# Cross-attention and low-rank FFN in one launch: the seam between the two stages rebuilt, weights split earlier, first and last tiles reordered

## What is computed

```
x = x + softmax(clip((LN(x) Wq + bq)(ctx Wk + bk)^T * 32**-0.5, +-10000)) (ctx Wv + bv) Wo + bo
x = x + gelu(LN(x) U1 V1 + b1) U2 V2 + b2        # U1 512x128, V1 128x2048, U2 2048x128, V2 128x512
```

## Time and profile before

| | |
|---|---|
| median of 3 runs | 580.68 us (578.64 to 581.20) |
| profiled execution | 577.34 us, span 575.5 us |
| mean granted PE clock | 0.997 |
| busy share of the span | PE 96%, PEld 81%, DVE 84%, POOL 64%, ACT 54% |
| moved by DMA | 50.36 MB |

### The profile page before, as it was taken

The page is one execution under the profiler, slowest core; times in us unless marked ns, Lnnn a source line. Parts: engine busy times, 40 slices in busy tenths (PEclk is TensorE's granted clock), DMA queues, the critical chain, the costliest instruction groups (busy, mean ns, idle before and its releaser), DMA issues.

```text
span 575.5 us, 11999 instructions
## 1 busy us (share of the span) xinstructions
PE 554.8 (96%) x4804; PEld 464.2 (81%) x4804; DVE 482.8 (84%) x697; ACT 308.7 (54%) x510; POOL 366.6 (64%) x286
## 2 busy tenths in 40 slices
PE   8999999999999999999987997999999999999996
PEld 8787878888988898888865675888888888888884
DVE  4778989888988898888779968888979797978675
ACT  3464454445444545444456543757575766666652
POOL 2787767777676777677565564757566656565561
PEclk9999999999999999999989999999999999999999
DMA  8422353222323123220412431012121212101012
GB/s 311 163 79 75 110 202 112 93 70 71 101 92 112 54 77 112 92 75 20 148 56 74 129 112 72 0 75 73 74 73 67 81 56 91 57 19 56 18 61 86
DMA packets 25263, 50.36 MB, mean 87 GB/s; under 512 B 2936, under 2 KB 3064, under 8 KB 24824
## 3 DMA queue, kind: packets, MB, share of 16 engines
q1 hardware_dynamic: 24920, 49.07, 24.8%
q10 hardware_dynamic: 288, 0.52, 0.3%
HBM read 32.49 MB, written 16.78 MB: 86 GB/s over the span
## 4 chain that ended last, share of the span: by engine, by line
PE 78%; DVE 9%; DMA 6%; ACT 2%; POOL 2%; issue 2%; SPq 1%; POOLq 0%; DVEq 0%
PE bank L965 46%; PE ps_s L965 15%; PE bank L1040 5%; PE ps_s L1014 4%; PE bank L1056 4%; DMA xs<-in_x 4%; PE bank L1081 2%; PE bank L986 2%; DVE ss L748 1%; DVE smax L757 1%; DVE ssum L762 1%; DMA fw<-y_between 1%; DVE stats L687 1%; POOL ss L399 1%; DVE hs_r L824 1%
## 5 line engine op out<-in xcount | busy, mean ns | idle before, releaser
L471 POOL TENSOR_TENSOR hs_r<-ss,hs_r 128x512 fp32r<-128x512 f32 x63 | 90.3, 1434 | 90.1 <-ACT hs_r L667 89.5
L646 ACT ACTIVATE ss<-ps_s,once 128x512 f32<-128x512 f32 x128 | 87.9, 689 | 67.5 <-PE ps_s L965 64.0
L965 PE MATMUL ps_s<-p1t_r,v_r 128*128 128x512 f32 x384 | 112.2, 401 | 0.3 <-DVE p1t_r L813 0.3
L965 PE MATMUL bank<-hs_r,u_r 128*128 128x512 f32 x384 | 109.3, 393 | 0.7 <-DVE hs_r L824 0.7
L399 POOL TENSOR_TENSOR ss<-ss,smax 128x1232 f32<-128x1232 f32 x32 | 75.1, 2346 | 49.6 <-DVE smax L757 49.5
L965 PE MATMUL bank<-zt_r,wqo_r 128*128 128x256 f32 x768 | 98.7, 284 | 1.1 <-DVE zt_r L708 1.1
L965 PE MATMUL bank<-wqo_r,ot_r 128*128 128x512 f32 x384 | 98.9, 407 | 0.7 <-DVE ot_r L770 0.5
L965 PEld LDWEIGHTS bank<-zt_r,wqo_r 128*128 128x128 f32 x768 | 92.5, 188 | 2.8 <-DVE zt_r L708 1.3
L965 PEld LDWEIGHTS bank<-hs_r,u_r 128*128 128x128 f32 x384 | 72.0, 188 | 17.9 <-DVE hs_r L824 1.1
L965 PEld LDWEIGHTS bank<-wqo_r,ot_r 128*128 128x128 f32 x384 | 70.9, 191 | 16.6 <-DVE ot_r L770 0.9
L407 POOL TENSOR_TENSOR ss<-ss,rsum 128x1024 f32<-128x1024 f32 x32 | 61.5, 1922 | 35.7 <-DVE rsum L764 35.5
(11 more groups left out here) (86 smaller groups left out, 817.9 us busy)
## 6 DMA issues: line engine op xcount, KB each, us to landing
xs<-in_x SPq DMA_DIRECT2D x64, 256.0 KB, 3.5
y_between<-xs SPq DMA_DIRECT2D x32, 256.0 KB, 2.0
xs<-y_between SPq DMA_DIRECT2D x4, 1024.0 KB, 5.9
fw<-y_between SPq DMA_DIRECT2D x4, 1024.0 KB, 5.6
out<-xs SPq DMA_DIRECT2D x16, 256.0 KB, 2.0
out<-fw SPq DMA_DIRECT2D x16, 256.0 KB, 2.0
ss<-in_wq SPq DMA_DIRECT2D x2, 512.0 KB, 8.1
xs<-in_Wo SPq DMA_DIRECT2D x1, 1024.0 KB, 9.5
```

The source lines that it names most:

```text
L471: pool.tensor_tensor(hs[:, c % 4, 1, :], hg[:, c % 4, :], hs[:, c % 4, 0, :].bitcast(F32), ALU.subtract)\
L646: act.activation(hg[:, c % 4, :], ps_s[:, c % 4, :], ACT.Gelu_apprx_tanh, bias=b1_c[:, c:c + 1]).then_inc(h_gelu, 1)
L965: mm = pe.matmul(ps, lhs(a), rhs(c), start=first and i == 0, stop=last and i == len(PASSES) - 1)
```

## The change

- **FFN weights.** `load_ffn` is issued behind `load_x` in tile 3 (before: ahead of it). V1 and U2 are split in eight pieces of 512 columns: `uv_high(i)` on ACT at the end of tiles 4 to 11, `uv_low(i)` on POOL in tiles 5 to 12, between `x_plus_bo` and `subtract_max` of the second half. U1 and V2 are split in tile 14: high parts on ACT, low parts on POOL (`u1_v2_low`) behind `normalise`. DVE splits no weights any more.
- **y.** `y_ring` is turned: blocks 0 and 1 go to the halves of `fw`, loaded in tile 12 once all eight pieces are split; block 2 goes to `xa`, loaded in tile 14; block 3 to `xb`.
- **The seam.** Tiles 14 and 15 and what follows are written out (`last_tiles`) on PE, ACT and DVE. The first two `norm_stats2` move to tile 13, `rstd2_of(0, 0)` and the four `norm_z2` to tile 14; the `turn_z2` are spread between the products of tile 15, the first ahead of `turn_probs`. On ACT the copies of the probabilities go ahead of an exponential. The last `project_out` writes another bank (`o_bank`), so it doesn't wait for the `y_sum` before it. `turn_z2` of block 1 waits for all `y_sum`.
- **First tiles.** `norm_stats` of tile 2 moves behind two `clip`/`maxima` pairs; `norm_z(1, 0)` on ACT and `rstd_of(1, 0)` on POOL move back; the first `scores` starts when half of q is there; `weigh_values` of tile 0 no longer waits for `zt_lo`.
- **The end.** In the last block `y_plus_b2` runs at chunks 1, 3, 5 and 9. The last U2 chunk and the last V2 products issue their passes with the high part first (`project_last_v2`).

Cut to its core:

```diff
-        y_ring = [xa, fw[:, 0:UB * D].rearrange("p (t d) -> p t d", t=UB),
-                  fw[:, FF:FF + UB * D].rearrange("p (t d) -> p t d", t=UB), xb]
+        y_ring = [fw[:, 0:UB * D].rearrange("p (t d) -> p t d", t=UB),
+                  fw[:, FF:FF + UB * D].rearrange("p (t d) -> p t d", t=UB), xa, xb]
+        o_bank = lambda j, b, u: B6 if is_block(NA - 1, j, b) and u else B7
+        LAST_ADDS = (1, 3, 5, 9)
...
+                    if there(NA, j, b, 3) and not (is_block(0, j, b) or is_block(1, j, b)):
+                        load_x(*shift(j, b, 3))
                     if is_block(3, j, b):
                         load_ffn()
-                    if there(NA, j, b, 3) and not (is_block(0, j, b) or is_block(1, j, b)):
-                        load_x(*shift(j, b, 3))
+                    if is_block(UV0 + NUV, j, b):
+                        sp.wait_ge(uv_lo, NUV)
+                        for k in range(4):
+                            sp.wait_ge(y_out[k], 16 * (TB // TA))
+                        load_y(0, 0)
+                        load_y(0, 1)
...
+            def uv_low(i):
+                hi, lo, src = uv_piece(i)
+                pool.wait_ge(uv_hi, i + 1)
+                pool.tensor_tensor(lo, src, hi.bitcast(F32), ALU.subtract).then_inc(uv_lo, 1)
...
# POOL, tile n = 2 * j + b
-                    if is_block(NA - 1, j, b):
+                    if is_block(NA - 2, j, b):
                         rstd2_of(0, 0)
+                    if 0 <= 2 * j + b - UV0 - 1 < NUV:
+                        uv_low(2 * j + b - UV0 - 1)
                     if there(NA, j, b, 0):
                         subtract_max(j, b, 1)
                         normalise(j, b, 0)
+                    if is_block(NA - 2, j, b):
+                        u1_v2_low()
...
# DVE, last_tiles: tile 14, then 15
+                clip(j, 0, 0)
+                maxima(j, 0, 0)
+                norm_stats2(0, 0, 2)
+                norm_stats2(0, 0, 3)
+                y_sum(j - 1, 0, 0)
+                clip(j, 0, 1)
+                maxima(j, 0, 1)
+                sums(j, 0, 0)
+                for t in range(UB):
+                    norm_z2(0, 0, t)
+                y_sum(j - 1, 0, 1)
+                heads_low(j - 1, 1)
+                turned_z2(0, 0, 0)
+                sums(j, 0, 1)
+
+                clip(j, 1, 0)
...
# PE, last_tiles: tile 15
+                scores(j, 1, 0)
+                turn_z2(0, 0, 0)
+                turn_probs(j, 0, 0, (0, 1))
+                project_out(j - 1, 1, 0)
+                turn_z2(0, 0, 1)
+                turn_probs(j, 0, 0, (2,))
+                scores(j, 1, 1)
+                turn_probs(j, 0, 1, (0, 1))
+                turn_z2(0, 0, 2)
+                turn_probs(j, 0, 1, (2,))
+                project_out(j - 1, 1, 1)
+                turn_z2(0, 0, 3)
+                weigh_values(j, 0)
...
# PE, project_last_v2
+                high(0)
+                high(1)
+                pe.wait_ge(q2_lo, NB)
+                low(0)
+                low(1)
+                for t in range(2, UB):
+                    high(t)
+                    low(t)
```

More of the change, by code:

```diff
@@ L337, in body2 @@
                 for b in range(2):
-                    if there(NB, j, b, 2):
+                    if there(NB, j, b, 2) and not is_block(0, j, b):
                         load_y(j + 1, b)
@@ L647, in gelu, with body @@
                                bias=b1_c[:, c:c + 1]).then_inc(h_gelu, 1)
+            def body(j):
+                if j == 0:
+                    first_tiles()
+                    return
+                if j == NA // 2 - 1:
+                    last_tiles()
+                if j >= NA // 2 - 1:
+                    return
+                for b in range(2):
+                    before, after = there(NA, j, b, -1), there(NA, j, b, 1)
+                    for u in range(2):
+                        if u == 0 and after:
+                            q_copy(*shift(j, b, 1), 0)
+                        if before:
+                            copy_probs(*shift(j, b, -1), u, (0, 1))
+                        if u == 1 and after:
+                            q_copy(*shift(j, b, 1), 1)
+                        if before:
+                            copy_probs(*shift(j, b, -1), u, (2,))
+                        if u == 0:
+                            exponent(j, b, 0)
+                    turned_z(j + 1, b)
+                    exponent(j, b, 1)
+                    if before:
+                        heads_high(*shift(j, b, -1))
+                    if 0 <= 2 * j + b - UV0 < NUV:
+                        uv_high(2 * j + b - UV0)
@@ L892, in body @@
-                    if there(NA, j, b, 2):
-                        turned_z(j + 1, b, (1,))
-                    if is_block(NA - 1, j, b):
-                        turned_z2(0, 0, 0)
-                        turned_z2(0, 0, 1)
-                    if here and not is_block(NA - 1, j, b):
-                        sums(j, b, 1)
-                    if is_block(NA, j, b):
-                        norm_stats2(0, 1, 0)
-                        norm_stats2(0, 1, 1)
-                    if before:
-                        heads_low(*shift(j, b, -1))
@@ new lines, in body, with last_tiles @@
+                    turned_z(j + 1, b, (1,))
+                    sums(j, b, 1)
+                    heads_low(*shift(j, b, -1))
+            def last_tiles():
+                j = NA // 2 - 1
+                clip(j, 0, 0)
[10 more added lines that the diff above has]
+                heads_low(j - 1, 1)
+                turned_z2(0, 0, 0)
+                sums(j, 0, 1)
+                clip(j, 1, 0)
+                maxima(j, 1, 0)
+                turned_z2(0, 0, 1)
+                y_sum(j - 1, 1, 0)
+                clip(j, 1, 1)
+                maxima(j, 1, 1)
+                turned_z2(0, 0, 2)
+                sums(j, 1, 0)
+                y_sum(j - 1, 1, 1)
+                turned_z2(0, 0, 3)
+                sums(j, 1, 1)
+                heads_low(j, 0)
+                p1_low(0, 0)
+                norm_stats2(0, 1, 0)
+                y_sum(j, 0, 0)
+                norm_stats2(0, 1, 1)
+                norm_stats2(0, 1, 2)
+                h_split(0, 0, 0)
+                norm_stats2(0, 1, 3)
+                y_sum(j, 0, 1)
+                heads_low(j, 1)
+                h_split(0, 0, 2)
+                y_sum(j, 1, 0)
+                y_sum(j, 1, 1)
@@ L1047, in weigh_values @@
                 pe.wait_ge(pt_copied, 6 * n + 6)
-                if there(NA, j, b, 3):
+                if there(NA, j, b, 3) and not is_block(0, j, b):
                     pe.wait_ge(zt_lo, 2 * (n + 3) + 1)
@@ L1178, in body @@
                     return
+                if j == NA // 2 - 1:
+                    last_tiles()
+                if j >= NA // 2 - 1:
+                    return
                 for b in range(2):
[L1180 removed]
+                    before, after = there(NA, j, b, -1), there(NA, j, b, 1)
                     for u in range(2):
[L1182 to L1183 removed]
+                        scores(j, b, u)
                         if u == 0 and after:
```

303 lines of the change are left out of this document (152 added, 151 removed).

## The result

| | before | after |
|---|---|---|
| median of the runs | 579.66 us (577.88 to 581.20, 4 runs) | 563.43 us (563.35 to 564.06, 4 runs) |
| profiled execution | 577.34 us, span 575.5 | 563.44 us, span 561.6 |
| mean granted PE clock of that | 0.997 | 1.0 |

The ratio is 0.973 with a 95% interval of 0.9703 to 0.9757: 2.7% faster, 16.2 us in the medians and 13.9 us between the two profiled executions.

What follows compares the result with a forecast made beforehand. PE's order of work was taken to bound the kernel, so only its lost time counts: 1.25 + 1.3 + 2.7 + 3.35 + 1.5 = 10.1 us off a 580.68 us median gives 570.6 us, range 566.8 to 574.6.

Steps and rivals of the forecast that it cites:

- Tile 3: Loading x ahead of the four FFN weights removes PE's wait for a low part of z: -1.3 us.
- FFN block 0: With y loaded earlier, PE's idle time after the end of attention goes whole: -3.35 us, bounds 2.5 to 3.4.
- the end: Last FFN block: earlier y_plus_b2 and high passes first shorten PE's last waits: -1.5 us, bounds 0.8 and 1.6.
- The middle tiles: Eight weight pieces on ACT and POOL fit into idle time, POOL keeping about 0.6 us: 0 us.
- the seam's: Tile 15 to the end of attention: waits and clock loss go from 7.4 to 4.7 us, a gain of 2.7.
- a wait of 2.1 us: Tile 15: PE waits 2.1 us for heads_low, since norm_z2 on DVE takes turns with POOL's instructions.
- a clock that falls again: Behind PE's wait in tile 15 the clock drops again, costing 1.7 us, 0.3 of it hidden: 1.4.
- the clock holds: Rival: in tile 15 the spread-out turn_z2 bridge the wait enough; 11.5 us gained, 569.2 us; chance 0.27.
- The bound of -5.5: Largest gain allowed from tile 15 to the end of attention, if DVE isn't held up and the clock holds.
- The median of the runs stands 3.3 us higher: Whole kernel: the median's offset over the profiled execution, 3.3 us, was carried over, giving 570.6 us instead of 567.2.
- first tiles: Tile 0: weigh_values starts earlier without its wait for an unused low part: -1.25 us, bounds 0.9 and 1.5.
- The table load: First GELU after attention: load of 1.28 us; a possible extra 1.4 us drain would lengthen PE's last wait there.

Runs made afterwards that it cites:

- the kernel with POOL held back: The changed kernel with the low parts of U1 and V2 on POOL held back until the four norm_z2 are done; median 563.09 us.
- the 29 runs: Runs of the unchanged kernel before, made beside the follow-up kernels and shared by four of them; 580.05 us.

## Why the prediction was wrong

**What held.** The bound (PE's waits, 5.7 + 1.7 + 3.4 us of them in the seam) was read rightly, and each wait that was to go went: tile 0's, tile 3's, the one for y, the one ahead of the last U2 chunk. Tile 3 gave 1.41 for 1.3, FFN block 0 2.95 for 3.35 (waits of 0.26 and 0.17 us stay), the end 1.2 for 1.5 (PE still waits 0.69 us for q2, where it waited 1.41). The middle tiles paid nothing for the pieces, and POOL's gap there is the 0.66 us that was forecast as about 0.6.

**The step that failed** is the seam's: "If they take turns like that, the four end at 289.9, 292.3, 293.4 and 295.1", and out of it a wait of 2.1 us and a clock that falls again: 2.7 us of gain where 6.6 came. The turns are real, as the kernel with POOL held back shows: without the two low parts beside it DVE saves 0.96 us. The Trainium skill's rule on the shared port pair (SBUF — State Buffer, "SBUF: two separate sides") fits that on DVE's side, which waits for the whole POOL instruction; POOL loses less (0.17 to 0.23 us) than one `norm_z2` takes on DVE with POOL idle (1.91 / 4 = 0.48 us, the last row below). The size of one turn was wrong. The earlier trace rows had it from both sides: `subtract_max` at 2.48 instead of 2.25 grew by 0.23 us, and the second `norm_z` ended at 243.09 + 2.93 = 246.02, only 0.28 behind `subtract_max` (243.26 + 2.48 = 245.74). So did two rows of the kernel before that the forecast left out, four `norm_z2` beside one `subtract_max`; the third is the changed kernel's next four, with POOL idle:

```profile
305.10 3.84 DVE L801 TENSOR_SCALAR once<-xs,mv_b,rstd_b 128x512 f32<-128x512 f32 x4
305.26 2.48 POOL L399 TENSOR_TENSOR ss<-ss,smax 128x1232 f32<-128x1232 f32 x1
...
328.62 1.91 DVE L840 TENSOR_SCALAR once<-fw,mv_b,rstd_b 128x512 f32<-128x512 f32 x4
```

With 0.2 a turn the four end 1.2 us earlier and the wait is 0.9, near the 0.79 measured. That error decided a second term: with waits of 0.79 and 1.08 us the clock stayed up in that place, with 1.98 it mostly fell. So 1.3 us of the wait took 1.4 us of clock with it. The rival named for this case, "the clock holds", gave a reason that isn't enough (the transposes bridge): with the same transposes a wait of 1.98 did bring it down. Whether they help at shorter waits is not shown; without them ahead of it a wait of 1.38 passed in the profile, and one run of four had a fall.

Of the seam's 6.57 us, 3.96 are waits (5.66 to 1.70), 1.7 the clock, and 0.9 lie inside what the view counts as PE's busy time (39.21 - 1.7 = 37.5 against 36.60). Against the forecast that is 1.6 us more of waits, 1.4 of clock and these 0.9. I had taken PE's own work as unchanged, and it is: 355 instructions in both. But PE's rows run on for 0.07 to 0.25 us into the next row wherever PE isn't held up, and at a wait this tail stands by itself and counts as busy. The seam had eight waits and has three; my estimate from the rows is tails of some 1.3 us before and 0.5 after, so about 0.8 of the 0.9 are the price of stopping five times more. No run tests this by itself. The bound of -5.5 was too near as well: by the forecast's own terms the seam without the wait of 2.1 and with the clock up gains 7.4 - 1.2 = 6.2. And where the forecast says that 1.7 us pass at the lower clock, 1.7 us is the loss; the clock was low for twice that.

**The second failed step** is "The median of the runs stands 3.3 us higher, at 580.68; there the forecast is 580.68 - 10.1". The 3.3 us were carried over as if they were a property of the measurement. Over the 29 runs the offset is 2.7 us (580.05 - 577.34), and the larger part of it is falls of the clock: 2.2 in a run of the kernel before on average, one in its profiled execution, so 1.2 x 1.6 = 1.9 us. The rest, up to 1 us, stays open: the ten runs with one fall average 578.35, the profiled execution with one took 577.34. Traces of the kernel before and its near variants show the falls in three places, all behind a wait of PE: tile 15 (1.59 us), FFN block 0 (3.3 and 3.4 us) and the first tiles (1.44 us). The change shortens all three waits (to 0.79, 0.26 and 0.43 us), so its median (563.43) is the time of its profiled execution (563.44), and its runs lie within 0.7 us where those of before spread over 6.3. Of the miss of 7.2 us, 3.3 are this offset and 3.9 the seam's; the other terms nearly cancel (first tiles 0.5 and tile 3 0.1 too little, FFN block 0 0.4 and the end 0.3 too much).

**The table load.** The Trainium skill (ScalarE: Activation LUTs, "What ACT_TABLE_LOAD costs") adds a drain of about 1.4 us. Here it does not show: the load starts at 312.37, 0.02 us after the copy ahead of it ends, and takes 1.28, the GELU starts at 313.66, and PE's wait was 0.63 against a forecast of 0.8 without the drain. The trace of the kernel before had it already: the load of 324.39 takes 1.28 and its GELU starts at 325.68.

## What to carry to other kernels

When runs of one kernel spread by a per cent and the profiled one is at the fast end, look at the granted clock of every run before carrying the offset over to a forecast: here the longer waits of PE (1.44 to 3.43 us in the traces that show it) put a second price of 1.6 us on themselves in some runs, and removing the wait paid both. When DVE and POOL hold each other up, the rows show both sides: take the length of DVE's turn from how much POOL's instruction grew and from how long after it DVE's ended, not from DVE's duration alone. And an idle gap ahead of an instruction is only a lower bound of its slack; double the suspected work and see.

## What the runs showed of the hardware

- In one place, behind `scores` and four transposes, a wait of PE of 0.79 or 1.08 us left the clock at 2.4 GHz, one of 1.98 us brought it to 1.2 GHz in two of three runs and one of 3.17 us in four of four. Elsewhere the same wait did it in one profile and not in another: 1.59 us in three of four, 3.2 to 3.4 us in three of five. In the profiles the clock stayed low for about 3.4 us, once for 6.8, and that cost half of it.
- A `norm_z2` of 128x512 fp32 from SBUF to SBUF on DVE holds POOL up for 0.17 to 0.23 us, and waits itself until POOL's current instruction is done; four of them took 1.91 us with POOL idle, 3.84 beside one POOL instruction of 2.48, 4.36 beside three and 5.32 beside four and the start of a fifth.
- 22 memsets of 128x1 on DVE took 0.33 us from the start of the first to the end of the last.
